# Attention's prologue: where the output weights' low parts, the next row's transposes and Pool's rope sums stand

## The reference

```
q = rope(heads(layernorm(x) @ Wq, 32)); k = rope(heads(layernorm(x) @ Wk, 8)); v = heads(layernorm(x) @ Wv, 8)
scores = q @ k^T / sqrt(32); scores[key later than query] = min float
x = x + (softmax(scores) @ v) @ Wo
x = x + autocorrelation(layernorm(x), ctx)          # per head: 2*log(L) best delays
x = x + mixing(layernorm(x))                        # sinkhorn of 50 iterations on 4x4
```

## Time and profile before

| | us |
|---|---|
| median of three runs | 1227.65 |
| lowest and highest | 1225.66, 1228.12 |
| profiled execution, its own time | 1224.81 |
| its span in the trace | 1223.0 |
| TensorE busy | 1026.1 (84%) |
| VectorE busy | 925.1 (76%) |
| ScalarE busy | 596.9 (49%) |
| Pool busy | 447.3 (37%) |

### The profile page before, as it was taken

One profiled execution on the slowest core, in us unless ns is written; L12 is line 12 of the kernel. 1 busy time (PEld: TensorE's weight loads), 2 busy tenths in 40 slices (PEclk: granted clock), 3 DMA queues, 4 the chain that ended last, 5 costly groups with the idle time before them and its releaser, 6 DMA issues. The chain is left out here.

```text
span 1223.0 us, 23230 instructions
## 1 busy us (share of the span) xinstructions
PE 1026.1 (84%) x7866; PEld 759.6 (62%) x7866; DVE 925.1 (76%) x2818; ACT 596.9 (49%) x1789; POOL 447.3 (37%) x620
## 2 busy tenths in 40 slices
PE   5599999999999999999666999999999896624056
PEld 4487777877777877777544677776565554323034
DVE  6766876666886666786523787787999999997994
ACT  6434555444555444555415677777556465212023
POOL 2524433234433333433313666664353343101020
PEclk9899999999999999999878999999999998757579
DMA  9010111111011111011122222332233211139025
GB/s 379 30 42 35 42 58 58 58 41 41 34 58 58 58 41 49 26 59 42 42 84 108 87 74 91 97 107 91 74 95 108 74 57 40 30 109 365 0 52 138
DMA packets 47234, 95.71 MB, mean 78 GB/s; under 512 B 5952, under 2 KB 30400, under 8 KB 47168
## 3 DMA queue, kind: packets, MB, share of 16 engines
q1 hardware_dynamic: 47168, 94.91, 23.2%
HBM read 64.48 MB, written 27.26 MB: 75 GB/s over the span
## 5 line engine op out<-in xcount | busy, mean ns | idle before, releaser
L614 POOL TENSOR_TENSOR prob_G<-prob_G,rl 128x512 f32<-128x512 f32 x96 | 99.8, 1041 | 258.5 <-DVE rl L502 258.5
L384 ACT ACTIVATE prob_G<-prob_G,negm 128x128 f32<-128x128 f32 x384 | 148.8, 389 | 89.6 <-DVE negm L444 89.6
L244 PE MATMUL ps_qkv<-w_hi,xT_hi 128*128 128x512 f32 x384 | 156.3, 407 | 12.6 <-DVE prob_G L507 8.6
L245 PE MATMUL ps_qkv<-w_lo,xT_hi 128*128 128x512 f32 x384 | 151.3, 394 | 0.0
L246 PE MATMUL ps_qkv<-w_hi,xT_lo 128*128 128x512 f32 x384 | 150.9, 393 | 0.0
L316 PE MATMUL ps_qkv<-wo_hi,aT_hi 128*128 128x512 f32 x256 | 108.0, 422 | 0.0
L318 PE MATMUL ps_qkv<-wo_hi,aT_lo 128*128 128x512 f32 x256 | 102.1, 399 | 0.0
L317 PE MATMUL ps_qkv<-wo_lo,aT_hi 128*128 128x512 f32 x256 | 102.1, 399 | 0.0
L244 PEld LDWEIGHTS ps_qkv<-w_hi,xT_hi 128*128 128x128 f32 x384 | 72.9, 190 | 38.4 <-issue 16.5
L440 DVE TENSOR_TENSOR prob_G<-ps_s,mask 128x512 f32<-128x512 f32 x96 | 64.9, 676 | 41.6 <-PE ps_s L227 41.1
L469 DVE TENSOR_TENSOR xT_lo<-ps_t,xT_hi 128x512 fp32r<-128x512 f32 x16 | 11.1, 692 | 103.1 <-ACT xT_hi L423 103.1
(11 more groups left out here) (252 smaller groups left out, 2663.3 us busy)
## 6 DMA issues: line engine op xcount, KB each, us to landing
xin<-in_x SPq DMA_DIRECT2D x16, 512.0 KB, 3.5
xres<-in_x SPq DMA_DIRECT2D x16, 512.0 KB, 5.3
x<-xres SPq DMA_DIRECT2D x16, 512.0 KB, 2.6
c_xin<-x SPq DMA_DIRECT2D x16, 512.0 KB, 4.4
c_b_xres<-x SPq DMA_DIRECT2D x16, 512.0 KB, 3.2
rows_x<-c_row SPq DMA_DIRECT2D x64, 128.0 KB, 2.3
m_xm<-rows_x SPq DMA_DIRECT2D x16, 512.0 KB, 8.5
out<-m_ot SPq DMA_DIRECT2D x64, 128.0 KB, 2.3
```

The source lines that it names most:

```text
L244: nc.tensor.matmul(ps_qkv[:, n, :], xT_hi[:, k, :], w_hi[:, k, cols], start=k == 0, stop=False)
L245: nc.tensor.matmul(ps_qkv[:, n, :], xT_hi[:, k, :], w_lo[:, k, cols], start=False, stop=False)
L384: r = nc.scalar.activation(prob(g)[:, j, :], prob(g)[:, j, :], ACT.Exp, bias=negm[:, h:h + 1], accum_out=lsum[:, h:h + 1])
L614: nc.gpsimd.tensor_tensor(prob(g), prob(g), rl[:, g * GROUP:(g + 1) * GROUP].rearrange("p (j o) -> p j o", o=1).to_broadcast([P, GROUP, T] ...
```

## The change

Four edits.

1. Pool makes four wo_lo pieces instead of five, all of them behind its three rope sums of `body(-1)`. The roots and sums no longer stand behind a piece.
2. VectorE makes the other four pieces instead of three. They leave `body(-1)`, where they stood ahead of the first `row_negm`, and stand in `body(0)` between the eighth block transpose and `rope_part(1)`. They count on a semaphore of their own, `wo_lo_by_dve`. TensorE's output matmuls of the first row wait for Pool's four pieces ahead of the first four k and for VectorE's four ahead of the others.
3. In `body(-1)` TensorE turns the next row ahead of keys and queries, and ScalarE copies `xT_hi` ahead of keys, queries and values (the copy of values was ahead of it too).
4. In `body(-1)` VectorE does `rope_part(0)` ahead of `norm_apply` instead of behind it.

```diff
--- before.py
+++ after.py
@@ -106,7 +106,7 @@
         AV = 4 * STRIPS
         BLK = P // STRIPS
         PARTS = (2, 0, 1)
-        WO_BY_POOL = 5
+        WO_BY_POOL = 4
         xT_bank = (ps_t[:, :], ps_s[:, 3, :])
 
         const_in = sem("const_in")
@@ -120,6 +120,7 @@
         w_lo_done = sem("w_lo_done")
         wo_hi_done = sem("wo_hi_done")
         wo_lo_done = sem("wo_lo_done")
+        wo_lo_by_dve = sem("wo_lo_by_dve")
         stat_step = sem("stat_step")
         rstd_done = sem("rstd_done")
         xn_done = sem("xn_done")
@@ -310,8 +311,10 @@
                             pe.wait_ge(al_done, 2 * b + G + 1)
                             if G == 0 and project:
                                 pe.wait_ge(rope_done, 3 * c + 2 + n)
-                            if first:
-                                pe.wait_ge(wo_lo_done, KD)
+                            if first and G == 0:
+                                pe.wait_ge(wo_lo_done, WO_BY_POOL)
+                            elif first:
+                                pe.wait_ge(wo_lo_by_dve, KD - WO_BY_POOL)
                         cols = slice(n * HALF, (n + 1) * HALF)
                         nc.tensor.matmul(ps_qkv[:, n, :], aT_hi[G][:, j, :], wo_hi[:, k, cols], start=k == 0, stop=False)
                         nc.tensor.matmul(ps_qkv[:, n, :], aT_hi[G][:, j, :], wo_lo[:, k, cols], start=False, stop=False)
@@ -339,6 +342,9 @@
                     project_run(23, 1)
                     weigh_values(1)
                     output_chunks(0, 0, GROUP)
+                if norm and project and not attend:
+                    x_transpose(0)
+                    x_transpose(1)
                 if project:
                     qk_transpose(0)
                     qk_transpose(1)
@@ -346,7 +352,7 @@
                     output_chunks(1, 0, GROUP)
                 if project:
                     qk_transpose(2)
-                if norm:
+                if norm and (attend or not project):
                     x_transpose(0)
                     x_transpose(1)
                 if attend:
@@ -404,6 +410,15 @@
                         x1_square(b - 1, xres)
                     attend_out(0)
                     attend_out(1)
+                def row_turned():
+                    for half in range(2):
+                        act.wait_ge(xT_ps, 2 * (b + 2) + half + 1)
+                        if project:
+                            act.wait_ge(qkv_ps, 3 * c + 3)
+                        nc.scalar.activation(xT_hi[:, 4 * half:4 * half + 4, :], xT_bank[half], ACT.Copy).then_inc(xh_done, 1)
+
+                if norm and project and not attend:
+                    row_turned()
                 if project:
                     if attend:
                         act.wait_ge(a_ps, 2 * AV * (b + 1))
@@ -415,12 +430,8 @@
                     act.wait_ge(qkv_ps, 3 * c + 1)
                     act.wait_ge(rope_done, 3 * c + 1)
                     nc.scalar.activation(v_rel[:, 0, :], ps_qkv[:, 2, KVW:2 * KVW], ACT.Copy).then_inc(v_done, 1)
-                if norm:
-                    for half in range(2):
-                        act.wait_ge(xT_ps, 2 * (b + 2) + half + 1)
-                        if project:
-                            act.wait_ge(qkv_ps, 3 * c + 3)
-                        nc.scalar.activation(xT_hi[:, 4 * half:4 * half + 4, :], xT_bank[half], ACT.Copy).then_inc(xh_done, 1)
+                if norm and (attend or not project):
+                    row_turned()
                 if project:
                     for g in range(STRIPS):
                         exponentials(b + 1, g)
@@ -525,6 +536,11 @@
                         norm_stats()
                     transpose_blocks(6)
                     transpose_blocks(7)
+                    if first:
+                        for k in range(WO_BY_POOL, KD):
+                            dve.wait_ge(wo_hi_done, k + 1)
+                            nc.vector.tensor_tensor(wo_lo[:, k, :], wo_raw[:, k, :], wo_hi[:, k, :].bitcast(F32),
+                                                    ALU.subtract).then_inc(wo_lo_by_dve, 1)
                     if project:
                         rope_part(1)
                     attend_out(0)
@@ -536,18 +552,16 @@
                 else:
                     if norm:
                         norm_stats()
+                    if project:
+                        rope_part(0)
+                    if norm:
                         norm_apply()
                     if project:
-                        for i in range(3):
+                        for i in range(1, 3):
                             rope_part(i)
                 if norm:
                     x_lo(0)
                     x_lo(1)
-                if project and not attend:
-                    for k in range(WO_BY_POOL, KD):
-                        dve.wait_ge(wo_hi_done, k + 1)
-                        nc.vector.tensor_tensor(wo_lo[:, k, :], wo_raw[:, k, :], wo_hi[:, k, :].bitcast(F32),
-                                                ALU.subtract).then_inc(wo_lo_done, 1)
                 if project:
                     for g in range(STRIPS):
                         row_negm(b + 1, g)
@@ -626,15 +640,12 @@
                         nc.gpsimd.tensor_tensor(wo_lo[:, k, :], wo_raw[:, k, :], wo_hi[:, k, :].bitcast(F32),
                                                 ALU.subtract).then_inc(wo_lo_done, 1)
 
-                if project and not attend:
-                    split_output_weight(0, 1)
                 if norm and not attend:
                     norm_rstd()
                 if project and not attend:
-                    split_output_weight(1, 2)
                     for i in range(3):
                         rope_sum(i)
-                    split_output_weight(2, WO_BY_POOL)
+                    split_output_weight(0, WO_BY_POOL)
                 elif project:
                     for i in range(1, 3):
                         rope_sum(i)
```

## The result

The changed kernel takes 1223.73 us (median of 13 runs, 1221.51 to 1226.06), against 1226.44 us of the kernel before in the same runs (13, 1224.54 to 1228.12). The ratio is 0.9977, with a 95% interval of 0.9969 to 0.9984: 2.7 us lie between the medians, 2.8 by the ratio, where 5.2 were forecast. The profiled execution took 1223.23 us, its span 1221.4, against 1224.81 and 1223.0. Busy times: VectorE 921.5 us instead of 925.1 although it has a piece more, Pool 442.5 instead of 447.3 with a piece less; what VectorE lost is time in which an instruction waited for Pool's.

The account below looks back on a forecast made before the run. TensorE, busy 39.36 of 40 us in the attention loop, was taken as the bound, so an earlier start stays won. 7.3 us at step 23 less 2.1 for half clock gave 5.2: 1222.4 against the 1227.65 median, range 1219.1 to 1226.0.

Parts of the forecast that it names:

- A: The forecast itself: 5.2 us won from the first output matmuls on, 1222.4 us, range 1221.5 to 1223.8; chance 0.50.
- the prediction's own signs of being wrong: Pool's products release VectorE, pieces exceed 1.3 us, or the lead at the first output matmul is gone at the end.
- Parts 1 to 3: Prologue: first scores 38.15 against 44.00, first mask 39.5 against 49.72; Pool's four pieces end at 46.0, late products hidden.
- Part 4: Second scores: TensorE idle 2.2 us only, full clock kept; VectorE's chain up to rope_part(0) moves 10.8 us earlier.
- Part 5: First attention body: VectorE's four pieces cost 4.6 us; step 23 at 65.65 against 72.93, 7.3 earlier, after a 4.6 gap.
- Part 6: TensorE's new gap: clock falls to half at or just after 65.6, costing 1.2 to 2.6 us; 2.1 taken.
- The sum: 7.3 us won at step 23 less 2.1 for the clock: 5.2 us earlier from the output matmuls at 75.21 on.
- B: Clock stays up at TensorE's new gap, or falls already near 44: 6.7 to 7.3 us won, 1220.3 to 1221.0; chance 0.25.
- C: Shared cost on VectorE or Pool, slower pieces or late products: 1.8 us won, 1225.9, or 1223.8 at full clock; chance 0.15.
- D: Slower: VectorE's four pieces each meet a Pool instruction and take 3.42 us, 13.7 together: 1231.5 us; chance 0.04.
- E: Edit swallowed: the start moves, but later waits between the phases take it back, 1227.6 us; chance 0.06.

Follow-up runs that it names:

- after: The changed kernel with all four edits, in its first profile, against the kernel before: 1223.73 us, ratio 0.9977.
- after_again: The changed kernel unchanged, run and profiled a second time, against the kernel before: 1224.62 us, ratio 0.9989.
- after_logs_first: The changed kernel with ScalarE's logarithms of chain b ahead of its output copies in the mixing phase: 1217.30 us, ratio 0.9936 to the kernel before.
- mixing_filled: The changed kernel with 14 unread matmuls in TensorE's wait for the first mixing rows: 1222.32 us, ratio 0.9961 to the kernel before.
- the logarithms first: ScalarE's chain b logarithms moved ahead of its output copies in both kernels: 1217.30 us changed, 1220.02 us before, 2.7 us apart.
- the second series: The follow-up runs with the changed kernel unchanged beside the kernel before: 1224.62 us, ratio 0.9989.
- pieces_early: The changed kernel with VectorE's four wo_lo pieces back in body(-1), ahead of the first row maxima: 1224.93 us, ratio 0.9988 to the kernel before.

## Why the prediction was right, and where its size was off

The median of 1223.7 lies in the range (1219.1 to 1226.0), 1.3 above the forecast. That it is so near is in part luck. The forecast started from three runs of before with a median of 1227.65, and the thirteen have 1226.44; from there 5.2 us less would have been 1221.2, 2.5 below what was measured. The gain was forecast about twice as large as it is. The range's upper end doesn't follow from its own terms either: A's 1223.8 and 1.2 for the spread give 1225.0, not 1226.0. The median lies under both.

One of the prediction's own signs of being wrong came true: the lead at the first output matmul, 5.2 us in the two first profiles, isn't there at the end, where their spans differ by 1.6.

**Parts 1 to 3, to the first mask: right.** From the first projection matmul on, 22.9 was forecast for the first scores and came in after, after_again and after_logs_first. In mixing_filled, with the same prologue, it was 23.6: the clock rose to full only 6.2 us behind the first projection matmul, against 2.8 to 4.4 us in those three. For the first mask 24.3 was forecast, measured 24.2 and 24.8 (the latter with the clock's fall in the scores), and 4.6 for VectorE's four pieces, measured 4.59. Pool's pieces ended at 45.6 as its bound of 2.31 each had it, and its late products stayed hidden. norm_apply took 0.81, not the 1.4 I expected, which changed nothing.

**Part 4: nearly.** I took full clock up to the second scores. In after it fell in the first scores already, for 3.4 us; it cost 0.6 at the mask. In after_again it didn't.

**Part 5: right.** Step 23 was forecast 50.4 behind the first projection matmul, after a gap of 4.6 that al_done ends; measured 50.9 and 50.3, after 4.3.

**Part 6, the clock behind the gap: right in kind, too small in size.** It fell at the gap's end, in after_again within it. I put 2.1 us down for it, from half clock of 2.7 to 6 us; it lasted 6.6, 8.2, 8.7 and 9.3 in the four profiles with this prologue, and filling the gap gave back 3.6. The sum's second mistake is tied to that: I let the lead stand as it was at the first output matmul (54.8 forecast, 54.8 and 54.3 measured), but half clock went on under the output matmuls behind it. At the end of attention the lead over the profile of before was 4.2 and 3.9, not 5.2.

**What before was, the step that I didn't see.** I measured the lead against one profile of before, whose attention stretch is 584.8. Two more have 583.6 and 583.5, with less half clock behind the second scores. Means of three each, 584.0 and 580.8, give a lead of 3.1; with mixing_filled, the fourth profile of the changed prologue, it is 2.7. Of the 5.2 that were forecast, 1.5 are the half clock behind the gap, priced too low (2.1 for 3.6), and 0.8 the profile of before. 2.9 are left, against measured 2.8 by the ratio, 2.7 with the logarithms first, and 1.3 by the ratio in the second series. That the last is lower isn't explained. The medians there rest on runs that spread over 4.2 and 6.5 us, and in after_again's profile the untouched stretch behind attention took 504.6 us, 1.1 to 1.8 more than in the three of before. The split is of the attention phase alone; that it meets the medians so well is in part chance, as the phases behind it differ by more from one execution to the next.

**The rivals.** A had the place and the mechanism, but its own range (3.9 to 6.1 won) was too high for the 2.7 won. B didn't come: the clock fell in both profiles. C had 1.8 us won, which is nearer to the measured 2.7 than A's 5.2 (though as a time its 1225.9 is farther off than A's 1222.4), but its cause is shown not to be there: the pieces took 1.15 each and Pool's products delayed nobody. D didn't come, and pieces_early shows when its price of 3.4 us a piece is paid: when Pool works on pieces at the same time. E was half right in a way that I hadn't meant: a later phase can swallow or add 2.6 us, but by the clock's chance, and in both kernels. The Trainium skill, "SBUF — State Buffer", section "Who interferes with whom", says that an instruction of VectorE with two SBUF inputs and one of GpSimd that reads SBUF block each other for their whole length. The trace agrees: here it was 3.35 to 3.38 us for an instruction of 1.15 beside one of 2.34, and 4.59 for four when Pool was idle.

## What to carry to other kernels

The edits were worth 2 to 3 us together. With the order of the transposes undone, or with two of Pool's pieces back ahead of the sums, all of it was gone; with VectorE's pieces back ahead of the masks about half of it was left in the attention phase. On a chain the gain of one link shows only if the others are in place, and what is moved off it has to land where its engine is idle, not merely later. Against the version with the pieces behind `attend_out(1)`, the same four instructions cost the attention phase 9.8 us ahead of the masks, where Pool works on its own, and 8.0 ahead of `aT_lo` (4.3 of idle time and about 3.6 of half clock). Less than 6 us further on they stand in VectorE's idle time.

When a wait moves to TensorE, price the half clock behind it up to where it ends, not to the next mark; and before a lead of a few microseconds is read from two profiles, take several of each kernel and see how much the stretches that nobody touched differ: here by up to 4.7 us.

## What the runs showed of the hardware

- TensorE's granted clock fell at the end of a gap of 4.3 us in one execution and 2.2 us into it in another of the same program, and stayed at half for 6.8 and 10.2 us. It also fell with no gap over 1.3 us just before: at the first scores in after, behind 1.27 and 0.69 us idle with short transposes between. In after_again, at the same place, it didn't fall.
- Half clock on an engine that isn't the bound made a stretch of the mixing phase up to 2.8 us longer in one profile than in another (65.5 and 68.3), and up to 4.1 longer than without the first spell of it (64.2): TensorE's outputs came later, ScalarE's copies of them too, and VectorE waited for the logarithms behind the copies.
- In the untouched stretch of 501.5 to 506.2 us behind attention, half clock lasted between 86 us (the shortest stretch) and 102 us (the longest).
- A VectorE subtraction of 128x1024 with both inputs in SBUF took 1.15 us beside an idle Pool and 3.38 beside Pool's own.
